# A fused attention and expert kernel: the feed-forward q and k projected once a batch and spread by DMA, with all steps in a new order

## The reference, cut to what matters

```
xn = layernorm(x)
attention (16 heads of 64, causal):  q, k, v = xn @ W_qkv; rotary on q and k;
    a = softmax(q k^T / 8, causal) v;  y = a @ W_out
feed-forward branch, on xn:
    q = xn @ Wq + bq;  k = xn @ Wk + bk;  v = xn @ Wv + bv     (16 heads of 8)
    ctx = softmax(q k^T / sqrt(8)) v                            (not causal)
    x2 = xn + layernorm(ctx @ Wo + bo) * g1 + be1
    gates = softmax(x2 @ Wg + bg), the two largest of 8 experts
    moe = sum of the two picked (x2 @ We[e] + bexp[e]), weighted
    f = x2 + layernorm(moe) * g2 + be2
out = x + y + f
```

## Time and profile before

| what | value |
|---|---|
| median of 3 timed runs | 1271.35 us |
| lowest and highest | 1267.77 and 1273.54 us |
| span of the profiled execution, first to last instruction | 1270.3 us |
| busy: PE, DVE, ACT, POOL | 91%, 73%, 70%, 64% |
| instructions | 25325 |

### The profile page before, as it was taken

The page is one execution under the profiler, slowest core; times in us unless marked ns, Lnnn a source line. Parts: engine busy times, 40 slices in busy tenths (PEclk is TensorE's granted clock), DMA queues, the critical chain, the costliest instruction groups (busy, mean ns, idle before and its releaser), DMA issues.

```text
span 1270.3 us, 25325 instructions
## 1 busy us (share of the span) xinstructions
PE 1159.3 (91%) x9387; PEld 741.3 (58%) x9387; DVE 928.0 (73%) x2336; ACT 892.0 (70%) x1841; POOL 811.5 (64%) x730
## 2 busy tenths in 40 slices
PE   4779999999999999999999999999999999899986
PEld 3355565655666565655656556665656556575655
DVE  7666487885878857896687848787687866778546
ACT  3567867487766868578775887668776796748860
POOL 3655774577855767568864778467675587645760
PEclk8799999999999999999999999999999999999998
DMA  4000100011000110001100011001000011000000
GB/s 144 34 34 18 43 35 17 26 39 38 34 18 26 51 43 26 18 26 59 39 13 35 26 43 42 18 26 51 34 29 24 25 35 51 18 17 34 34 18 9
DMA packets 34110, 42.87 MB, mean 34 GB/s; under 512 B 5694, under 2 KB 17216, under 8 KB 33988
## 3 DMA queue, kind: packets, MB, share of 16 engines
q1 hardware_dynamic: 30516, 38.31, 8.2%
q10 hardware_dynamic: 3472, 2.95, 0.8%
HBM read 5.60 MB, written 2.10 MB: 6 GB/s over the span
## 4 chain that ended last, share of the span: by engine, by line
PE 59%; DVE 17%; ACT 14%; issue 4%; POOL 4%; DMA 1%; SPq 0%; ACTq 0%; DVEq 0%; POOLq 0%
PE work L1319 7%; PE work L1233 7%; PE work L1334 6%; PE work L1346 6%; PE work L1235 6%; PE work L1234 6%; PE work L1396 5%; DVE fnmax L1071 5%; ACT fpt L884 5%; PE work L1362 4%; ACT pn L926 4%; DVE work L1193 3%; PE work L1371 3%; PE work L1386 3%; ACT pt L938 2%
## 5 line engine op out<-in xcount | busy, mean ns | idle before, releaser
L926 ACT ACTIVATE pn<-work,nmax 128x512 f32<-128x512 f32 (+3 forms) x512 | 265.3, 534 | 119.9 <-DVE nmax L1193 119.4
L785 POOL TENSOR_TENSOR raw<-raw,cos_t 128x512 f32<-128x512 f32 x128 | 163.8, 1280 | 284.9 <-DMA swapped<-raw 269.7
L1071 DVE TENSOR_REDUCE fnmax<-work 128x2 f32<-128x1024 f32 x256 | 302.0, 1219 | 47.0 <-PE work L1371 45.8
L1193 DVE CUSTOM_DVE_ANT_0 work<-work,causal 128x512 f32<-128x512 f32 (+3 forms) x512 | 236.1, 520 | 95.5 <-PE work L1319 94.7
L884 ACT ACTIVATE fpt<-work 128x1024 f32<-128x1024 f32 x256 | 252.4, 1029 | 52.7 <-PE work L1386 51.4
L1334 PE MATMUL work<-consts,pn 128*128 128x128 f32 x1280 | 172.6, 277 | 7.0 <-DVE fnmax L1071 4.0
L789 POOL TENSOR_TENSOR raw<-raw,swapped 128x512 f32<-128x512 f32 x128 | 163.7, 1279 | 10.0
L1334 PEld LDWEIGHTS work<-consts,pn 128*128 128x128 f32 x1280 | 141.1, 141 | 42.7 <-DVE fnmax L1071 13.0
L800 POOL TENSOR_TENSOR qk_l<-raw,qk_h 128x512 fp32r<-128x512 f32 x128 | 163.3, 1282 | 2.8
L786 POOL TENSOR_TENSOR swapped<-swapped,sin_t 128x512 f32<-128x512 f32 x128 | 163.7, 1279 | 0.0
L938 ACT COPY pt<-work 128x1024 f32<-128x1024 f32 x128 | 130.4, 1019 | 42.6 <-PE work L1334 42.1
(11 more groups left out here) (161 smaller groups left out, 2140.1 us busy)
## 6 DMA issues: line engine op xcount, KB each, us to landing
swapped<-raw SPq DMA_DIRECT2D x256, 128.0 KB, 2.0
x_in<-in_L_attn_x_dram SPq DMA_DIRECT2D x8, 256.0 KB, 3.4
out_dram<-x_in SPq DMA_DIRECT2D x7, 256.0 KB, 2.2
fpt<-in_L_attn_W_qkv_dram ACTq DMA_DIRECT2D x3, 512.0 KB, 5.9
pt<-in_L_ffn_We_dram ACTq DMA_DIRECT2D x1, 512.0 KB, 7.2
wout<-in_L_attn_W_out_dram ACTq DMA_DIRECT2D x1, 512.0 KB, 8.4
out_dram<-x_in SPq DMA_DIRECT2D x2, 128.0 KB, 1.8
pt<-in_rope_dram ACTq DMA_DIRECT2D x1, 192.0 KB, 6.5
```

The lines of the kernel that those rows point to most:

```text
L785: nc.gpsimd.tensor_tensor(raw[:, n % 3], raw[:, n % 3], cos_t[:], ALU.mult)
L926: ins = nc.scalar.activation(pn[:, h, PN_AT[j]:PN_AT[j] + n], bank_of(("sc", b, c, unit), h)[:, at:at + n], ACT.Exp, scale=-1.0, bias=nmax ...
L1071: nc.vector.tensor_reduce(fnmax[:, j, 2 * r:2 * r + 2, 0:1], bank_of(("fsm", b, g, j), 2 * r, 2).rearrange("p (f n) -> p f n", f=2), AX.X, ...
L1193: ins = nc.vector.tensor_tensor_reduce(out=scores, in0=scores, in1=causal[:, S - n:S], scale=-1.0 / math.sqrt(DH), scalar=3.0e38, op0=ALU.add,
```

## The change

- **fqk once a batch.** q and k of all 16 heads are projected in their own order, 128 rows, with 2 x 3 matmuls. The bias is a column (qk_bias, loaded as it is). fqkh and fqkl write high and low parts into fqn (four rows of 512: q high, q low, k high, k low), once a batch.
- **fdup(b,g)**, a new step on SP: three transfers of 128 KB copy group g's 32 partitions of fqn into places 1, 2 and 3 of the strips fqs (partitions c, c+4, ... now, a ring of two). It waits for fqkl(b) and for fst of two groups before. fsm waits for its landing; fqkh of the next batch waits for the landing of all copies of the one before. Place 0 is set once at the start to 0 and 1.
- **fsub** writes q with its maxima into a tile of its own, fqm, and so waits for fst of the group before.
- **l_rows goes.** fan writes l_wide, rT reads it, rb writes the turned form over it, so fan(c) waits for div(c-1).
- The strips' weights, their clearing and the turned bias at the start go; fqk stands ahead of proj there.
- **Order.** START and its kin are replaced by PLACE, which gives each step of each batch its place in its engine's list, and PSUM gives banks batch by batch. On PE a step (the fqk apart) moves by 0.56 places on average, at most 8; on ACT 0.69, on DVE 0.74, on POOL 1.65, on SP 0.34.

The diff, cut to its core:

```diff
+        def landed(kind, *key):
+            n = key[0] * G + key[1]
+            return (fdup_done[n % 2], 16 * 3 * (n // 2 + 1)) if n >= 0 else (begun, 1)
...
+                elif kind == "fdup":
+                    g = x_[2]
+                    wait(sp, after("fqkl", b))
+                    wait(sp, after("fst", *ring(2, b, g, G), T - 1))
+                    for c, pair in ((1, slice(0, 4, 2)), (2, slice(1, 3)), (3, slice(0, 4, 3))):
+                        sp.dma_start(fqs[c:P:4, g % 2].bitcast(F32), fqn[g * STRIP:(g + 1) * STRIP, pair].bitcast(F32))                            .then_inc(fdup_done[g % 2], 16)
...
                 elif kind == "fqkh":
-                    g = x_[2]
-                    wait(act, after("fqk", b, g))
-                    wait(act, after("fst", *ring(2, b, g, G), T - 1))
+                    wait(act, after("fqk", b))
...
+                    wait(act, *(landed("fdup", b - 1, g) for g in range(G)))
+                    for k in range(2):
+                        ins = nc.scalar.activation(fqn[:, 2 * k], bank_of(("fqk", b), k), ACT.Identity, bias=qk_bias[:, k:k + 1])
...
                 elif kind == "fan":
...
-                    wait(act, after("rT", *ring(1, b, c, NC)))
-                    nc.scalar.copy(l_rows[:].rearrange("p (t h n) -> p t h n", t=T, h=2),
+                    wait(act, after("div", *ring(1, b, c, NC)))
+                    nc.scalar.copy(l_wide[:].rearrange("p (t h n) -> p t h n", t=T, h=2),
...
                 elif kind == "rb":
...
-                    wait(act, after("div", *ring(1, b, c, NC)))
...
+                        ins = nc.vector.scalar_tensor_tensor(out=fqn[:, 2 * k + 1], in0=bank_of(("fqk", b), k), scalar=qk_bias[:, k:k + 1],
+                                                             in1=fqn[:, 2 * k].bitcast(F32), op0=ALU.add, op1=ALU.subtract)
...
-                    nc.vector.tensor_tensor(fqk[:, g % 2, 0], bank_of(("fmT", b, g)), fqk[:, g % 2, 0].bitcast(F32),
-                                            ALU.add).then_inc(done["fsub"], 1)
+                    wait(dve, after("fst", *ring(1, b, g, G), T - 1))
+                    nc.vector.tensor_tensor(fqm[:], bank_of(("fmT", b, g)), fqs[:, g % 2, 0].bitcast(F32), ALU.add).then_inc(done["fsub"], 1)
...
                 elif kind == "fqk":
-                    g = x_[2]
-                    if g == 0:
-                        wait(pe, after("xl", b))
-                        if b == 0:
-                            wait(pe, after("strl", 0))
+                    wait(pe, after("xl", b))
+                    if b == 0:
+                        wait(pe, after("strl", 0))
                     for k in range(2):
-                        wh = strips_h[:, k, g * GH:(g + 1) * GH].rearrange("p h c -> p (h c)")
-                        wl = strips_l[:, k, g * GH:(g + 1) * GH].rearrange("p h c -> p (h c)")
-                        ins = split3(bank_of(x_, k), wh, wl, xt_h[:, b % 2], xt_l[:, b % 2])
+                        ins = split3(bank_of(x_, k), wqk_h[:, k], wqk_l[:, k], xt_h[:, b % 2], xt_l[:, b % 2])
...
                     if j == 0:
-                        wait(pe, after("fqkl", b, g))
+                        wait(pe, landed("fdup", b, g))
```

More of the change, by code:

```diff
@@ L54 @@
 LOADED = ("tt", "strl", "tb", "sml", "bia", "wel")
[L58 to L133, removed]
[10 rows of a table removed]
-    "max": [-88.756596, -88.475366, -88.41445, -86.778713, -84.135428, -83.881474, -71.249536, -70.505656, -65.714658,
[5 rows of a table removed]
-    "exp": [-53.078638, -52.39101, -51.71477, -49.728579, -48.940391, -47.123439, -18.594468, -17.329814, -4.382652,
[7 rows of a table removed]
-    "tpe": [-39.309081, -29.149792, -0.647223, 1.317237, 22.287919, 30.131276, 39.579323, 42.0214, 69.422546, 72.697422,
-        78.316275, 80.6584, 88.083511, 91.586633, 99.409889, 101.707729],
-    "tqe": [-82.092567, -57.592391, -42.295327, -26.30228, -8.001158, 13.726925, 28.393263, 59.175223],
-    "pv": [-149.325569, -145.219837, -119.323959, -109.733002, -98.689708, -85.946333, -81.719558, -46.1868],
-    "inv": [-77.84043, -61.775104, -55.631275, -31.124475, -1.839394, 14.67873, 28.043971, 59.181535],
-    "fan": [-44.888278, 0.249118, 19.54039, 40.752235, 71.969872, 79.527007, 86.74259, 99.955304],
-    "rT": [-167.54159, -148.533989, -126.7654, -110.160989, -101.367195, -88.784743, -82.775769, -59.612729],
[L165 to L168, removed]
@@ L464, in later @@
-def later(kind, b, n):
-    own = {0: FIRST, B - 1: LAST}.get(b, {}).get(kind)
-    return own[n] if own else SHIFT.get(kind, {}).get(b, 0)
+    "xT": ["6", "4", "0", "0", "0", "0", "0", "0"],
+    "tt": ["2"],
+    "proj": [
+        "4046707760166020", "0001407760106020", "5007500760106020", "0070506760106020", "0045401760106020",
+        "0075406760106020", "0007407760106020", "0077406760106020",
+    ],
+    "tb": ["7"],
+    "fqk": ["1", "4", "5", "5", "5", "5", "5", "5"],
+    "fv": ["7", "7", "7", "7", "7", "7", "7", "7"],
@@ new lines @@
+    "fsm": [
+        "4040402042402020", "4110402042402021", "4023222142402021", "4143202042402021", "4230202042402021",
+        "4120202042402021", "4132202042402021", "4132402042402021",
+    ],
+    "fmT": ["1474", "0524", "5104", "5704", "4074", "4525", "5704", "4374"],
+    "fst": [
+        "0420402014200344", "0420002444201343", "0031002344200344", "0420002444201344", "0420002344201343",
+        "0420002444200344", "0420002444201344", "0420002344201344",
+    ],
+    "fpv": ["6671", "6171", "7171", "6171", "6171", "6171", "6171", "6171"],
@@ L475 @@
     "POOL": ("rs0", "rs1", "rs2", "rope", "hi", "lo", "x2", "res", "out"),
-    "SP": ("swap", "store", "load"),
+    "SP": ("swap", "fdup", "store", "load"),
 }
+LAST_ON_DVE_STEPS = ("res_last", "out_last")
 KEYS = {}
-for kind in START:
+for kind in PLACE:
     if kind in ("ao", "yadd"):
@@ L485 @@
         KEYS[kind] = [(c, unit, h) for c in range(NC) for unit in range(3) for h in range(2)]
-    elif kind in ("fT", "fdiv", "fmT", "fo", "fqk", "fqkh", "fqkl", "fsub"):
+    elif kind in ("fT", "fdiv", "fdup", "fmT", "fo", "fsub"):
         KEYS[kind] = [(g,) for g in range(G)]
@@ L501 @@
         KEYS[kind] = [()]
-TIME = {(kind, b) + key: PERIOD * b + at + later(kind, b, n) for kind in START
-        for b in range(1 if kind in ONCE else B) for n, (key, at) in enumerate(zip(KEYS[kind], START[kind]))}
-for b in range(B - XB, B):
-    del TIME["load", b]
-LAST_ON_DVE = {"res": ("yadd", B - 1, 1), "out": ("nm2", B - 1)}
-for kind, x in LAST_ON_DVE.items():
-    del TIME[kind, B - 1]
-    TIME[kind + "_last", B - 1] = TIME[x] + 1e-3
-ORDER = {engine: sorted((x for x in TIME if x[0] in kinds), key=TIME.get) for engine, kinds in ENGINE.items()}
+BATCHES = {kind: [0] if kind in ONCE else [B - 1] if kind in LAST_ON_DVE_STEPS else range(len(rows)) for kind, rows in PLACE.items()}
+AT = {(kind, b) + key: at for kind, rows in PLACE.items() for b, row in zip(BATCHES[kind], rows) for key, at in zip(KEYS[kind], row)}
+LAST_ON_DVE = ("res", "out")
+ORDER = {engine: sorted((x for x in AT if x[0] in kinds), key=AT.get) for engine, kinds in ENGINE.items()}
 COUNT = {}
@@ L542, in place @@
             continue
-        homes = LAST_PSUM.get(x[0], PSUM[x[0]]) if x[1] == B - 1 else PSUM[x[0]]
-        i = first[x] = homes[[y for y in KEYS[x[0]] if x[0] != "fpv" or y[1] == 0].index(x[2:])]
+        homes = [y for y in KEYS[x[0]] if x[0] != "fpv" or y[1] == 0]
+        i = first[x] = int(PSUM[x[0]][x[1]][homes.index(x[2:])])
         before[x] = [y for y in holder[i:i + WIDE.get(x[0], 1)] if y is not None]
@@ L610, in build @@
         u = sb("u", [P, NC // 2, S])
-        fqk = sb("fqk", [P, 2, 2, S], F32R)
+        fqn = sb("fqn", [P, 4, S], F32R)
+        fqs = sb("fqs", [P, 2, 2, S], F32R)
+        fqm = sb("fqm", [P, S], F32R)
         fnmax = sb("fnmax", [P, T, GH, STRIP])
@@ L857, in _ @@
                     wait(act, after("proj", b - 2, NC - 1, 1))
-                    wait(act, after("fqk", b - 2, G - 1))
+                    wait(act, after("fqk", b - 2))
                     wait(act, after("v", b - 2, T - 1))
@@ L1385, in _ @@
                         r = slice(f * STRIP, (f + 1) * STRIP)
-                        ins = nc.tensor.matmul(bank_of(x_, f), fqk[r, g % 2, 1, tile(i)], fqk[r, g % 2, 0], start=True, stop=True,
+                        ins = nc.tensor.matmul(bank_of(x_, f), fqs[r, g % 2, 1, tile(i)], fqm[r], start=True, stop=True,
                                                tile_position=(r.start, 0))
```

891 lines of the change are left out of this document (581 added, 310 removed), and 302 rows, old and new, of tables (FIRST, LAST, LAST_PSUM, PLACE).

## The result

The changed kernel takes 1231.45 us (median of 4 runs, 1230.26 to 1236.28) against 1272.44 us of the kernel before (4 runs, 1267.77 to 1276.60): ratio 0.9686, interval 0.9651 to 0.9720, 41.0 us less. Measured once more beside the last experiments it took 1234.35 us (6 runs, 1229.04 to 1240.07), ratio 0.9687, interval 0.9654 to 0.9721. The forecast was 1236. The profiled execution took 1231.06 us, with a span of 1229.2.

A forecast was written before the change was run, and what follows sets the result against it. PE, busy 91% of the span, was taken to bound the kernel. The terms 41.1 - 2.4 - 1.1 - 4 + 2 = 35.6 us gave 1270.3 - 35.6 + 1.05 = 1235.8, forecast 1236; own range 1226 to 1247, overall range 1224 to 1257.

The forecast's parts named there:

- fqk once a batch, 41.1 us: On PE, 6 fqk matmuls a batch instead of 24: 34.3 us saved in seven batches, 6.8 in batch 0.
- Copies, 2.4 us, landing 2.0: SP's new copies land after 2.0 us like swaps; fsm of group 3 waits 0.3 us a batch, 2.4 in all.
- rival C: Copies land slower than swaps, at 3.05 us, costing 8 us more at group 3: 1244 us; chance 0.15.
- SP's queue has room: SP gains 12 copy issues, 7 us a batch, beside 19 us of swap issues, so its queue has room.
- POOL idles anyway: POOL, which waits for swaps, is idle 269.7 us already, so 1.8 us of delay at one swap costs nothing.
- New waits, 0: fsub's wait for fst (0 to 0.7 us a batch) and fan's for div (0 to 1.0) taken as 0.
- Start, +1.1: Before the first fsm, a split, swap issue and copy are added: about 24.1 us, +1.1 (-1 to +4).
- 4 us given back: Where PE gets shorter, waits for DVE and ACT give back 4 us of the saving.
- New order, 0 (-4 to +4): PE's steps move half a place on average, the tail likewise: 0 us, -4 to +4.
- the 2 us of the chain: Pieces of ACT and DVE work on the chain that go: 2 us saved.
- a lower granted clock in the middle: Sign that the forecast was wrong: a lower granted clock in the middle; no size given.
- PE's idle time over 10 us a batch: Sign that it was wrong: PE idle over 10 us a batch, with waits for DVE nmax or ACT pn.

The follow-up runs named there:

- the last experiments: Changed kernel with DVE's list reordered around its layer norms: division earlier in batches 1 to 3, 1229.00 us; subtraction of maxima earlier too in batches 4 to 7, 1226.84 us.
- experiment 1: Changed kernel with PE doing the six fqk matmuls of a batch four times over, 24 a batch as before the change: 1264.83 us, ratio 0.9955.
- experiments 3: All the changed kernel's work in the old kernel's order and PSUM banks, two steps moved so that it ends: 1295.46 us, ratio 1.0197.
- experiment 4: All the changed kernel's work in the old order and banks, with SP's list mended at two places, copies put behind a swap and a load: 1278.23 us, ratio 1.0034.
- experiment 5: Kernel before, with only the reciprocals' rows and turned form sharing one buffer and the last fan moved: 1276.13 us, ratio 1.0019.
- experiments 2: Kernel before, old order, with one fqk pass instead of three in groups 1 to 3, 12 matmuls a batch fewer: 1263.81 us, ratio 0.9952.
- experiment 7: Changed kernel with one of the three copies of a group, places 2 and 3 of the strips not written: 1233.19 us, ratio 0.9684.

## Why the prediction was right, and where it was not

The time and its sign were right (1236 against 1231.45, inside 1226 to 1247). Step by step:

- *fqk once a batch, 41.1 us.* Right: PE's busy time fell by 40.3, and what is put back (experiment 1) costs 33.4 us for matmuls of 33.6.
- *Copies, 2.4 us, landing 2.0.* They land after 2.7. But group 3 of the middle batches never waited for one; the 5.5 us of waits are one at the start, one at the second batch, one at the last. The landing lies between the forecast's 2.0 and rival C's 3.05; C's 8 us did not come.
- *SP's queue has room.* True of its sum and of the new order, false as an argument: the same issues at two worse places cost 17 us (experiments 3, 4). "POOL idles anyway" didn't cover a late swap, because rstd stood behind it, and the 269.7 us of idle time were POOL's waits for these very swaps.
- *New waits, 0.* Small: fan's costs about 2 us alone (experiment 5); DVE waited 13.5 us for the fst before fsub and 3.6 for fmT (9.8 for fmT before), PE 3.5 us for fsub.
- *Start, +1.1.* The first fsm came at 25.14 instead of 24.1, for the copy's landing: +2.1.
- *4 us given back.* The undisturbed period is 145.7, where I expected 144.6: 1.1 a batch more than the terms had, some 8 us.
- *New order, 0 (-4 to +4): the step that failed.* By place in time, with the 4 us given back and the 2 us of the chain put to the middle: the start gained 9.3 us where the terms had 5.4, the six stretches up to the last 15.1 where they had 25.6, the last and the drain 16.7 where they had 4.6. So the total is right in part by luck: too much in the middle and too little at the two ends offset each other. Of the ends, PE's idle time fell by 2.1 us in the last stretch and by 5.4 in the drain, 7.5 us. By the experiments its worth depends on the rest: 44 us with the new work (experiment 4 against the changed kernel), about 6 us with PE's old amount of work put back (experiment 1, ratio 0.9955). The change without its new order is 4 us slower than the kernel before, and the new order with the old load on PE gains 6; together they gain 41.
- *The clock.* No term had it. The forecast named a lower granted clock in the middle as a sign that it was wrong, and it came: two batches hold 10.2 us at the half clock each and last 4.5 us longer than the batch behind them (150.2 against 145.7). PE's idle time over 10 us a batch, another such sign, came in two batches (11.2 and 10.4).

Why the two need each other is shown only in part. What the traces show is that in the old order idle time grows when PE has less to do (111 to 126 to 149 us, experiments 2, 4). My reading, which no run tests, is that the old order was made for a PE that has 149 us to do in a batch with 141 of them busy, and that a PE that runs ahead arrives at maxima, exponentials and banks that come at the old time. Experiment 4 also has the new waits, fsub's above all, and 5.0 us of waiting for the first copy, so its 44 us aren't the order's alone under the old waits. Which entries of the order, or which banks, make them up wasn't taken apart.

## What to carry to other kernels

In an order fixed by hand, cutting work and ordering anew are one change: price a cut by asking, for each engine, what the next steps in its list wait for once the cut one is gone. An engine's idle sum is not slack at a place: look at what stands directly behind a waiting instruction in each in-order list, DMA queues too. And count how long a bank stays held, by the last reader and not by the engines' load. And where two kernels differ in order, compare the first and last batch apart from the middle ones.

## What the hardware showed

- Six runs of the changed kernel spread over 11 us, from 1229.04 at a granted clock of 0.976 to 1240.07 at 0.964; the kernel before spreads over 11 us too (1267.27 to 1278.36, 17 runs).
- Here PE idle in short pieces was followed by a stretch at the lower clock, 1.2 GHz, though PE was then busy. In the changed kernel, 3.04 us busy of 5 at full clock, with no wait over 1.43 us, then a granted clock of 0.62, 0.50 and 0.86; the batch with it took 150.1 us:

```profile
325.00:330.00 5.00, 3.04 (x27) 1.97 (x24) 4.17 (x6) 3.52 (x5) 4.76 (x6) 1.00 0.02 3
330.00:335.00 5.00, 4.89 (x28) 3.84 (x26) 2.59 (x3) 3.27 (x4) 1.03 (x2) 0.62 0.00 0
335.00:340.00 5.00, 5.00 (x26) 1.88 (x29) 1.90 (x12) 1.94 (x2) 2.14 (x2) 0.50 0.00 0
340.00:345.00 5.00, 4.76 (x31) 1.70 (x25) 3.29 (x7) 1.77 (x3) 1.76 (x3) 0.86 0.01 3
```

- The same step with the same gaps isn't always followed by it: in the run of experiment 7 the stretch behind 332 us shows 0.71 in one window of 5 us and then 1.00, and that batch took 147.0 us. In the profiled run of the changed kernel again the same gaps are followed by no low stretch at all, and it took 147.1; two later batches hold 13.7 and 10.2 us of it instead and take 151.1 and 149.0. So the same gaps cost 0 to some 4 us beyond themselves, from run to run.
- A copy within SBUF of 128 KB lands after 2.0 us from 64 partitions of all 128, 2.1 from every fourth, 2.6 to 2.7 from 32 neighbouring ones.
